# A recurrent layer with a mixture of experts on one core: 71 expert slots for 72, dispatches without a bounds check, labels ahead of ranks

## The reference

```
x  = x + attn(layernorm(x))
#   attn: xn = ln(x); k, v, r from mixes of xn and its shifted self
#         wkv: a = ew*a + exp(k)*v ; b = ew*b + exp(k) ; out a/(b+eps)   (scan over 256 tokens)
#         x = x + (sigmoid(r)*wkv) @ Wo
#         yn = ln(x); kk = relu((0.5 yn + 0.5 shifted yn) @ Wfk)**2
#         x + sigmoid(yn @ Wfr) * (kk @ Wfv)
xm = layernorm(x)
scores = xm @ gate.T                      # 8 experts
p1, p2 = softmax(top 2 scores)
h12 = xm @ w12[e].T ; h1, h2 = halves     # 256 each
y   = sum over the two experts of p * ((silu(h1)*h2) @ w3[e].T)
return x + y
```

## Time and profile before

| | |
|---|---|
| median of 3 runs | 309.73 us (309.21 to 310.80) |
| profiled execution | 308.16 us |
| its span, first to last instruction | 306.4 us |
| granted TensorE clock, mean | 0.948 |
| DMA, mean over the span | 95 GB/s |

### The profile page before, as it was taken

How to read it: one execution, slowest core, us unless ns; L and a number is a source line. 1 busy time by engine, 2 the same in 40 slices (tenths; PEclk the granted TensorE clock), 3 DMA queues, 4 the chain that set the end, 5 groups by cost and what they waited for, 6 DMA issues and landing times.

```text
span 306.4 us, 6391 instructions
## 1 busy us (share of the span) xinstructions
PE 256.2 (84%) x1726; PEld 209.0 (68%) x1726; DVE 231.2 (75%) x740; ACT 195.9 (64%) x412; POOL 210.6 (69%) x224
## 2 busy tenths in 40 slices
PE   4778599999879899895998997488998999999600
PEld 4634376776647566474687896488997999999500
DVE  2699998999889798899767567875667466666656
ACT  3657798888858888388496755165766566766100
POOL 5390635947787977979676787777777777776640
PEclk9999999999979999799899999599999999999955
DMA  7950000000111101111454112333522333433696
GB/s 234 433 200 0 3 0 34 3 35 26 41 40 36 66 32 40 37 38 68 100 111 109 54 52 72 100 77 92 137 69 72 100 103 96 107 98 125 234 291 251
DMA packets 22418, 29.23 MB, mean 95 GB/s; under 512 B 4317, under 2 KB 15583, under 8 KB 22128
## 3 DMA queue, kind: packets, MB, share of 16 engines
q1 hardware_dynamic: 14976, 16.60, 17.7%
q0 software_dynamic: 4352, 8.47, 8.0%
q10 hardware_dynamic: 3056, 3.76, 3.8%
HBM read 15.09 MB, written 12.14 MB: 89 GB/s over the span
## 4 chain that ended last, share of the span: by engine, by line
PE 34%; DVE 21%; issue 17%; POOL 15%; DMA 8%; ACTq 1%; SPq 1%; ACT 1%; POOLq 1%; DVEq 0%
PE p_up L865 12%; POOL rows_d L463 8%; DVE st L923 4%; DMA x_all<-x 3%; POOL res_d L480 3%; PE p_up L770 3%; PE p_f L886 3%; PE p_tok L886 3%; PE p_f L784 2%; PE p_up L727 2%; DMA o_raw<-res_d 2%; DVE p_up L986 2%; PE p_up L726 2%; POOL rs L412 2%; DVE num L979 2%
## 5 line engine op out<-in xcount | busy, mean ns | idle before, releaser
L463 POOL DMA_INDIRECT rows_d<-rows,pos x64 | 66.4, 1038 | 22.2 <-issue 22.2
L865 PE MATMUL p_up<-xgT,w_up 128*128 128x128 f32 x576 | 71.1, 277 | 1.1 <-DVE hid L1160 1.1
L865 PEld LDWEIGHTS p_up<-xgT,w_up 128*128 128x128 f32 x576 | 67.8, 193 | 1.4 <-issue 1.3
L480 POOL DMA_INDIRECT res_d<-yo,xg x48 | 47.3, 985 | 16.8 <-issue 15.6
L1156 DVE SCALAR_TENSOR_TENSOR gate_h<-th,p_up 128x512 f32<-128x512 f32 x36 | 24.7, 687 | 35.1 <-ACT th L635 34.2
L655 ACT ACTIVATE w_up<-w_exp 128x512 f32 x72 | 41.3, 622 | 2.3 <-issue 0.7
L635 ACT ACTIVATE th<-p_up 128x512 f32<-128x512 f32 x36 | 21.5, 596 | 30.5 <-PE p_up L865 29.6
L770 PE MATMUL p_up<-ysum,w_sb 128*128 128x512 f32 x64 | 33.4, 619 | 2.1 <-POOL ysum L442 2.1
L784 PEld LDWEIGHTS p_f<-wfv_half,kk 128*128 128x128 f32 x256 | 30.8, 192 | 3.9 <-issue 3.3
L784 PE MATMUL p_f<-wfv_half,kk 128*128 128x128 f32 x256 | 32.2, 277 | 0.0
L480 POOL DMA_INDIRECT res_d<-o_raw x24 | 23.4, 975 | 9.1 <-issue 6.3
(11 more groups left out here) (168 smaller groups left out, 539.0 us busy)
## 6 DMA issues: line engine op xcount, KB each, us to landing
xg<-rows_d SPq DMA_DIRECT2D x48, 65.0 KB, 2.0
w_exp<-experts SPq DMA_DIRECT2D x1, 3072.0 KB, 18.2
o_raw<-res_d SPq DMA_DIRECT2D x12, 256.0 KB, 4.9
x_all<-x SPq DMA_DIRECT2D x10, 256.0 KB, 2.3
o_raw<-rows_d SPq DMA_DIRECT2D x24, 65.0 KB, 1.9
x_all<-x SPq DMA_DIRECT2D x1, 1536.0 KB, 9.7
rows_d<-rows,pos POOLq DMA_INDIRECT x64, 2.4
o_raw<-res_d ACTq DMA_DIRECT2D x4, 256.0 KB, 7.3
```

The lines of the kernel that those rows point to most:

```text
L463: pool.indirect_dma_start(out=rows_d[:, :], out_offset=bass.IndirectOffsetOnAxis(ap=row, axis=0), in_=rows_of[c % 2][:, t, k, :], in_offse ...
L480: pool.indirect_dma_start(out=res_d[:, :], out_offset=bass.IndirectOffsetOnAxis(ap=row, axis=0), in_=yo[b][:, n, :], in_offset=None, bound ...
L865: mm = pe.matmul(p_up[b][:, n, h * P:(h + 1) * P], w_up[q % 2][:, n, h * P:(h + 1) * P], xgT[q % 2][:, n, :], start=True, stop=True)
```

## The change

Four things, none of which changes what is computed.

- The last pair has one slot. `width(q)` is 2 for all pairs but the last, for which it is 1, and every step of a pair works on `width(q)` slots: loads, turns, weights, up, tanh, gating, down, weighing, scatter. The waits for its semaphores and the table of awaited scatters follow: a constant table `all_written` (two fills on GpSimd at the start) and one more VectorE operation, a minimum.
- The 64 dispatches have no bounds check. GpSimd's two dispatch steps become four, one for each tile, in the same places.
- For the last two chunks VectorE does the first part of `label` (which expert has the higher number, and the label) ahead of `place`, and the shares directly behind `place`, ahead of `ln3`. For the other chunks `label` stays. ScalarE copies the rows of chunk 7 ahead of the exponential of the gap.
- Where weights are mixed and halved on ScalarE at the start is written into the steps instead of `woven`, at the same positions; the first steps of `late_table` are a step of their own, directly ahead of it.

```diff
+        def width(q):
+            return 2 if q < PAIRS - 1 else 1
+        def landed(q):
+            return 16 * (2 * ((q - EARLY_PAIRS) // BUFS) + width(q))
...
-                sp.load(row_numbers, slot_row[0:1, 2 * q:2 * q + 2])
+                sp.load(row_numbers[0:width(q)], slot_row[0:1, 2 * q:2 * q + width(q)])
...
-                for n in range(2):
+                for n in range(width(q)):
...
-            for u in range(BUFS):
-                sp.wait_ge(S[f"scattered{u}"], 32 * LATE_ROUNDS)
+            for q in range(PAIRS - BUFS, PAIRS):
+                sp.wait_ge(S[f"scattered{buffer_of(q)}"], landed(q))
...
+            pool.memset(all_written[:, :, :], float(32 * LATE_ROUNDS)).then_inc(S["consts"], 1)
+            pool.wait_ge(S["consts"], 10)
+            pool.memset(all_written[:, :, BUFS - 1:BUFS], float(landed(PAIRS - 1))).then_inc(S["consts"], 1)
...
-                            in_=rows_of[c % 2][:, t, k, :], in_offset=None, bounds_check=c + E * REGION, oob_is_err=False)\
+                            in_=rows_of[c % 2][:, t, k, :], in_offset=None)\
...
-                            (dispatch_first, 4), (ln2_power, 1), (dispatch_second, 4), (gate_sums, 0)], {(9, 4): [(scatter, 0)], (9, 5): [(scatter, 1)], (10, 0): [(scatter, 2)]})
+                            (dispatch_tile(0), 4), (dispatch_tile(1), 4), (ln2_power, 1), (dispatch_tile(2), 4), (dispatch_tile(3), 4), (gate_sums, 0)], {(9, 4): [(scatter, 0)], (9, 6): [(scatter, 1)], (10, 0): [(scatter, 2)]})
...
-                           (second_apply, 3), (gap_exp, 5), (exps, 1), (normed_y, 3), (copy_rows, 5),
+                           (second_apply, 3), (copy_last_rows, 5), (gap_exp, 5), (exps, 1), (normed_y, 3), (copy_first_rows, 5),
...
-            def label(c):
-                after(dve, "egap_ready", c + 1)
-                dve.tensor_scalar(esum[:, :], egap[:, :], 1.0, None, ALU.add).then_inc(S["esum_ready"], 1)
+            def number(c):
                 dve.tensor_tensor(higher[:, 0, :], low[:, 0, :], low[:, 1, :], ALU.is_lt)
...
+            def share(c):
+                rows = rows_of[c % 2]
+                after(dve, "egap_ready", c + 1)
+                dve.tensor_scalar(esum[:, :], egap[:, :], 1.0, None, ALU.add).then_inc(S["esum_ready"], 1)
+                after_dispatched(dve, c)
...
+            def number_late(c):
+                if c >= CHUNKS - 2:
+                    number(c)
+            def share_late(c):
+                if c >= CHUNKS - 2:
+                    share(c)
+            def label(c):
+                if c < CHUNKS - 2:
+                    number(c)
+                    share(c)
...
-                dve.tensor_scalar(last_scatter[:, :, :], rounds_used[:, :, :], 1.0, 32.0, ALU.max, ALU.mult)\
+                link(dve.tensor_scalar(written_up_to[:, :, :], rounds_used[:, :, :], 1.0, 32.0, ALU.max, ALU.mult))
+                dve.wait_ge(S["consts"], 11)
+                dve.tensor_tensor(last_scatter[:, :, :], written_up_to[:, :, :], all_written[:, :, :], ALU.min)\
                     .then_inc(S["table_used"], 1)
-            pipeline(dve, [(place, 4), (ln3, 3), (label, 4), (wkv_sums, 0), (ln3_apply, 3), (ln2, 1),
+            pipeline(dve, [(number_late, 4), (place, 4), (share_late, 4), (ln3, 3), (label, 4), (wkv_sums, 0), (ln3_apply, 3), (ln2, 1),
```

More of the change, by code:

```diff
@@ L464, in dispatch, with dispatch_tile, step @@
                             out=rows_d[:, :], out_offset=bass.IndirectOffsetOnAxis(ap=row, axis=0),
-                            in_=rows_of[c % 2][:, t, k, :], in_offset=None, bounds_check=c + E * REGION, oob_is_err=False)\
+                            in_=rows_of[c % 2][:, t, k, :], in_offset=None)\
                             .then_inc(dispatch_sem(c), 16)
[L468 to L472, removed]
+            def dispatch_tile(t):
+                def step(c):
+                    dispatch(c, [t])
+                return step
             def scatter(q):
@@ L634, in tanh @@
                 after(act, "gate_h_ready", q)
-                act.activation(th[:, :, :], p_up[up_of(q)][:, :, 0:H], ACT.Tanh, scale=0.5).then_inc(S["tanh_ready"], 1)
+                some = slice(0, width(q))
+                act.activation(th[:, some, :], p_up[up_of(q)][:, some, 0:H], ACT.Tanh, scale=0.5).then_inc(S["tanh_ready"], 1)
             def turned_rows(q):
@@ L650, in expert_weights @@
                     act.wait_ge(S["table_w"], 1)
-                act.load(loaded, slot_w[0:1, 2 * q:2 * q + 2])
+                act.load(loaded[0:width(q)], slot_w[0:1, 2 * q:2 * q + width(q)])
                 after(act, "up_done", q - 1)
-                for n in range(2):
+                for n in range(width(q)):
                     first_col = act.snap(loaded[n], min_val=0, max_val=(E - 1) * EW)
@@ L840, in turn_rows @@
                 else:
-                    pe.wait_ge(S[f"xg_loaded{buffer_of(q)}"], 32 * ((q - EARLY_PAIRS) // BUFS + 1))
+                    pe.wait_ge(S[f"xg_loaded{buffer_of(q)}"], landed(q))
                 after(pe, "xgT_ready", q)
@@ L869, in down @@
             def down(q):
-                pe.load(loaded, slot_w[0:1, 2 * q:2 * q + 2])
-                first_col = [pe.snap(value, min_val=0, max_val=(E - 1) * EW) for value in loaded]
+                pe.load(loaded[0:width(q)], slot_w[0:1, 2 * q:2 * q + width(q)])
+                first_col = [pe.snap(value, min_val=0, max_val=(E - 1) * EW) for value in loaded[0:width(q)]]
                 after(pe, "hid_ready", q + 1)
@@ L1155, in gate_hidden @@
                 b = up_of(q)
-                dve.scalar_tensor_tensor(out=gate_h[:, :, :], in0=th[:, :, :], scalar=1.0, in1=p_up[b][:, :, 0:H],
+                some = slice(0, width(q))
+                dve.scalar_tensor_tensor(out=gate_h[:, some, :], in0=th[:, some, :], scalar=1.0, in1=p_up[b][:, some, 0:H],
                                          op0=ALU.add, op1=ALU.mult).then_inc(S["gate_h_ready"], 1)
```

50 lines of the change are left out of this document (32 added, 18 removed).

## The result

The changed kernel takes 307.48 us against 309.27 (medians of 11 executions each, side by side): ratio 0.9942, 95% interval 0.9915 to 0.9969, so 1.8 us less, at the edge of what can be told. The profiled execution took 306.8 us with a span of 305.1. The forecast was 307.5.

The account below looks back on a forecast made before the run. GpSimd and VectorE alternate on the chain, GpSimd alone from chunk 4, with two TensorE stalls after. Gains 0.96 + 0.48 + 0.8 = 2.2 us give 306.0 from the profiled 308.16, 307.5 from the median; range 303.8 to 310.0.

Parts of the forecast that it names:

- The turn that was read: Stretch from 70 to 146 us: one 18.9 us turn, 8.0 of GpSimd with four of eight dispatches, then 10.9 of VectorE.
- From chunk 4 on GpSimd itself is the chain: No other engine breaks into its eight dispatches; the last sixteen run without a pause, one every 1.27 us.
- The dispatches: Dropped checks save 0.03 us each: 32 in chunks 0 to 5 give 0.96, sixteen more take 0.48 off stalls.
- the stalls: TensorE's waits for late pairs, 0.92 and 1.64 us, together 2.56; sixteen cheaper dispatches take 0.48 off them.
- The wait at pair 20: TensorE's 1.64 us wait for pair 20's load, held by pair 12's scatter; forecast near 1.2.
- a spacing of 1.24: Sign to check: dispatch spacing 1.24 by the forecast, 1.12, 1.27 and above 1.3 by first, second and third rivals.
- the second rival: Checks hidden under generation and tail limited by transfers: gain 0 to 1.2, time 309.1, spacing 1.27; chance 22%.
- Labels: VectorE's label operations ahead of ranks in chunks 6 and 7: cover and room absorb the shifts, worth zero.
- The single pair: Tail: pair 35 halved, up done and ScalarE's results loads issued 0.9 us earlier; gain 0.8, bounds zero to 0.9.
- The third rival: Unchecked form slower: preparation adds 0.1 us per GpSimd dispatch, 313.7 rather than 309.7; chance 10%.
- The first: Rival: check dear, comparing and masking 128 indices costs 0.15 per dispatch; gain 8.0, time 301.7; chance 20%.
- its own signs: Wrong if dispatch spacing changes by a tenth or more, or TensorE's half-speed clock falls in another place.

Follow-up runs that it names:

- the early counts: Changed kernel, with SyncE and ScalarE reading the awaited scatter counts while pairs are still under way: 307.09 us, ratio 0.9937 to the kernel before.

## Why the prediction was right, and where it wasn't

**What bounds it.** Half right. The turn that was read, 8.0 us of GpSimd and 10.9 of VectorE, is the one with TensorE at full clock; in the turns beside it TensorE is on the chain, as said above, and the prediction doesn't name it. In the turns the prediction put four dispatches of GpSimd on the chain and the other four beside VectorE "with little room". The room was nil: in the chain of the kernel before VectorE ends at 115.11 and the fourth dispatch of the first group, started at 114.12, at 115.09. So with a shorter chain all eight count, and so does what releases the first. "From chunk 4 on GpSimd itself is the chain" was wrong for its start. The first line is of the kernel before, the second of the changed kernel with labels as before:

```profile
147.19 1.04 POOL L449 TENSOR_TENSOR rs<-var,neg_half 128x4 f32<-128x4 f32 x1 [1.20 <-DVE var L1022]
```

```profile
146.35 1.04 POOL L461 TENSOR_TENSOR rs<-var,neg_half 128x4 f32<-128x4 f32 x1 [1.59 <-DVE var L1049]
```

GpSimd waits there for VectorE, and 0.39 of the gain is given back.

**The dispatches: 1.44 forecast, 2.1 measured (1.1 to 3.1).** The interval takes in the forecast; what shows that the working failed is the turns. The step that failed is the price, "I take the row nearest to what is removed, the move". Its 29 ns are its own time. Where the queue runs ahead, the spacing fell by 0.013 us (from 1.276 to 1.263), less than half of the 0.03; at a group's head, where it can't, 0.38 go (0.54 to 0.16) at the second group and 0.08 at the first. In a turn at full clock that makes 0.46 (0.47 measured in the turn with chunk 0's dispatches, 0.36 from 18.92 to 18.56) where 0.12 was forecast. Chunks 4 and 5, forecast with 0.48, gave nothing: from the last dispatch of chunk 3 to that of chunk 5 it is 41.07 us before, 41.51 after and 41.19 with labels as before. With the check gone alone it is even 42.24: GpSimd waits 1.26 us there for VectorE's `ffn` at 161.39, which gives back most of what its turns had won. Of the stalls the forecast had 0.48; the kernel with the check gone alone has 0.54 and 1.57 where the earlier trace rows have 0.92 and 1.64, and a new one of 0.23 at 241.70: 0.22 less in all. From the last dispatch to the end it has 98.9 us for 99.5. The wait at pair 20, forecast near 1.2, is 0.58 in the changed kernel and 1.29 when it is profiled again. The test named in the prediction, a spacing of 1.24, would have pointed to the second rival (1.27), though the kernel was faster: the spacing was the wrong place to look.

**Labels: zero forecast, a loss measured.** 0.8 us by themselves (0.0 to 1.7), and in the changed kernel 1.6 (307.09 to 305.50, one group, taking the early counts as worth nothing) to 2.2 (307.48 to 305.27, two groups; by their ratios, 0.9942 and 0.9856, it would be 2.7). The working treated chunks 6 and 7, where it holds, and there the move was free. It missed that `label` was also split and turned round for chunks 0 to 5, and that the first dispatch of a group waits for the last share. The profile before had put that wait to "issue".

**The single pair: 0.8 forecast, 1.4 measured (0.8 to 2.0).** The forecast lies on the edge of the interval, and the mechanism was right: from the start of pair 34's up to ScalarE's loads it is 9.3 us in the kernel before (281.51, 290.84) and 8.4 with the single pair alone (282.00, 290.41), the 0.9 forecast. VectorE has half of pair 35's work less too and comes to its adds sooner, which may be the rest, but no run shows what that is worth: 5.9 us after the start of the last up before, 3.8 with the single pair. From pair 34's up to the end the five kernels with a full pair 35 have 23.5 to 24.9 us, mean 24.1, the nine with a single one 22.4 to 23.4, mean 22.8: 1.3 us.

**The yardstick.** The prediction saw that the profiled execution lay 1.6 us under the median and added the difference back. The profiles suggest what it was. From chunk 1's gate product to chunk 2's the chain goes through TensorE, before and after, and this takes 12.23 us with a granted clock of 1.00 in the kernel before and in the single pair alone; 13.60 to 13.93 with 0.87 or 0.88 in most others, the changed kernel among them; 14.67 and 15.01 with 0.77 in two. The two profiled executions with the full clock there are the two that lie well under their medians (1.6 and 1.8). Adding the 1.7 us between them brings both to within 0.2 of their medians (an estimate). So spans of single profiles shouldn't be compared here. From chunk 2's product to the end it is 262.0 us before, 259.2 and 258.6 in the changed kernel's two profiles, 260.6 with the check gone alone, 260.3 with the single pair alone and 257.4 to 257.7 in the four with the old order in chunks 0 to 5; but 261.0 with the check on one only and 260.2 with it gone from one only, so half a microsecond or so of these is chance.

**Sum.** 2.2 forecast, 1.8 measured: -2.1 and -1.4 against 0.8 to 2.2 leave -1.3 to -2.7 by parts. So the total was hit by errors of opposite sign, which is luck, and not by its working. The third rival (unchecked slower) is excluded, 0.9931 ends below 1. The first (check dear, 0.15 for each dispatch, so 0.6 a turn) had the wrong mechanism, masking of indices, but was nearer to the 0.36 to 0.47 of a turn than the forecast's 0.12; the second was half right, in that inside groups the check is nearly hidden.

**What stays open.** By its own signs the prediction would be wrong if TensorE's half speed fell in another place, and it did: between the gate products of chunks 1 and 2, where the profile before had none, and in one of the three turns for two. It is open why the half-speed stretch falls in two of the three turns in four of the kernels above, in one of them in others and in none in the fastest. The new label order always has one; the old order has two, one or none, so it isn't one part of the change that decides, and what it is was not tried. A part of the 2 us that the label order costs may thus be the clock's. Why the kernel with the check gone from one dispatch gains 1.6 us in the turns of its profile and almost nothing in the median (0.9989) is open too. Nor were scatters without a check tried: rows of idle slots would then all need places of their own.

The fastest kernels here, 305.0 to 305.5 us (0.985 to 0.989), faster than both, are the changed one with the old label order in chunks 0 to 5.

## What to carry to other kernels

In this kernel a register operation that prepares an instruction was nearly free where the queue runs ahead (0.013 us); at the head of a group, behind a vector operation, it cost 0.38 us. So look for the idle time in front of it on the chain (0.31 us here) and price that, once for each such head. Before two profiles are compared, compare the granted clock of their stretches. When one engine's part of a loop gets shorter, list what had no slack beside it, and what releases it, for that becomes the next bound; idle time put to "issue" may be a wait for another engine, seen by a constant distance to that engine's last operation (here in chunks 1 to 4). And read a diff for what it does in the chunks that its description doesn't name.

## What the hardware did that was not expected

Successive dispatches start 1.276 us apart with the check (971 ns each in the median) and 1.263 without (958), and the 0.30 idle in between stays. Scatters, which keep their check in all kernels, start 1.276 us apart where the dispatches have one too and 1.288 where these have none: in the changed kernel each is some 10 ns longer (0.98 instead of 0.97), on an unchanged line. With the check gone from one dispatch in eight they stand at 1.286 and 1.283. So a change on 64 of the transfers lengthened the other 71 by 0.012 us each, 0.9 us of GpSimd. The cause wasn't looked for.
